# Letting the groups of an edge sort share lines by adding into zeroed memory

## The reference

```
h = emb; acc = emb                      # emb: 12501 x 128
for _ in range(2):
    h = segment_sum(adj_val[:, None] * h[adj_col], adj_row, num_segments=N)
    acc = acc + h
graph = acc / 3
combined = graph[items] + item_features[items]
seq_hidden = take_along_axis(combined, alias_inputs[..., None], axis=1)
... masked mean, tanh, sigmoid, a weighted sum: sess_emb (512 x 128)
scores = (12 * l2norm(sess_emb)) @ l2norm(graph).T
```

## Time and profile before

| | us |
|---|---|
| median of three runs | 4053.59 |
| the profiled execution | 4058.68 |
| its span, first to last instruction | 4056.9 |
| POOL busy | 2797.3 |
| DVE busy | 3050.2 |
| PE busy | 2694.8 |
| ACT busy | 810.4 |

### The profile page before, as it was taken

One profiled execution on the slowest core, in us unless ns is written; L12 is line 12 of the kernel. 1 busy time (PEld: TensorE's weight loads), 2 busy tenths in 40 slices (PEclk: granted clock), 3 DMA queues, 4 the chain that ended last, 5 costly groups with the idle time before them and its releaser, 6 DMA issues.

```text
span 4056.9 us, 81702 instructions
## 1 busy us (share of the span) xinstructions
PE 2694.8 (66%) x14549; PEld 2317.8 (57%) x14550; DVE 3050.2 (75%) x7307; ACT 810.4 (20%) x2729; POOL 2797.3 (69%) x2868
## 2 busy tenths in 40 slices
PE   4899999566656655655664666666556555665798
PEld 2777777455555555655554555555556555553454
DVE  8999999777777777776766677677677776777575
ACT  0899999100000000000000000000000000005453
POOL 2466767777777777777775777777777777775770
PEclk8888888777777777777777677777776777776798
DMA  1000000122222222222243222222222222243243
GB/s 36 3 4 3 3 3 3 51 56 56 56 54 54 55 56 53 56 55 54 56 109 110 56 56 55 56 55 56 56 55 55 55 55 54 55 118 103 61 154 143
DMA packets 153127, 231.39 MB, mean 57 GB/s; under 512 B 65824, under 2 KB 106168, under 8 KB 152568
## 3 DMA queue, kind: packets, MB, share of 16 engines
q0 software_dynamic: 89760, 164.71, 17.6%
q1 hardware_dynamic: 48140, 59.06, 4.7%
q10 hardware_dynamic: 14796, 3.77, 0.9%
HBM read 186.08 MB, written 41.29 MB: 56 GB/s over the span
## 4 chain that ended last, share of the span: by engine, by line
POOL 33%; DMA 24%; issue 22%; DVE 10%; PE 9%; ACT 2%; SPq 0%; ACTq 0%; DVEq 0%; POOLq 0%
POOL store L634 31%; DMA store<-in_L_rec_emb,store 13%; DMA store<-table,store 10%; PE bank L1661 2%; ACT big L708 2%; DVE store L980 1%; PE bank L1602 1%; POOL store L661 1%; DVE big L924 1%; PE bank L1689 1%; DVE big L940 1%; PE bank L1648 1%; DVE store L932 1%; POOL sorted_edges L590 1%; PE bank L1502 1%
## 5 line engine op out<-in xcount | busy, mean ns | idle before, releaser
L1602 PE MATMUL bank<-store,shared 128*128 x9952 | 1762.3, 352 | 1151.8 <-POOLq L619 809.8
L1602 PEld LDWEIGHTS bank<-store,shared 128*128 128x128 f32 x9952 | 1646.9, 260 | 1267.2 <-issue 1264.9
L1294 DVE TENSOR_TENSOR acc<-acc,bank 128x256 f32 x2488 | 1034.4, 416 | 812.9 <-PE bank L1602 797.1
L634 POOL DMA_INDIRECT store<-table,store x1146 | 1086.0, 948 | 388.9 <-issue 326.4
L634 POOL DMA_INDIRECT store<-in_L_rec_emb,store x1146 | 1084.7, 947 | 373.2 <-issue 328.4
L1244 DVE TENSOR_SCALAR shared<-bank,mlo,mval 128x256 f32<-128x256 f32 x2488 | 1340.0, 539 | 0.0
L724 ACT COPY mlo<-store 128x24 f32 (+1 forms) x104 | 21.9, 211 | 2845.2 <-PE bank L1602 2120.4
L708 ACT ACTIVATE big<-big 128x68 f32<-128x68 bf16 x1764 | 557.4, 406 | 0.0
L1502 PE MATMUL bank<-big,store 128*128 128x136 f32 x2352 | 438.6, 326 | 57.4 <-DVE store L932 15.3
L590 POOL DMA_INDIRECT sorted_edges<-moved,block_to x313 | 401.5, 1283 | 101.7 <-issue 101.2
L1502 PEld LDWEIGHTS bank<-big,store 128*128 128x128 f32 x2352 | 351.6, 214 | 142.5 <-ACT big L708 122.2
(11 more groups left out here) (254 smaller groups left out, 1486.4 us busy)
## 6 DMA issues: line engine op xcount, KB each, us to landing
store<-in_L_rec_emb SPq DMA_DIRECT2D x3072, 0.5 KB
store<-in_L_rec_emb ACTq DMA_DIRECT2D x3072, 0.5 KB
store<-table SPq DMA_DIRECT2D x3072, 0.5 KB
store<-table ACTq DMA_DIRECT2D x3072, 0.5 KB
scores<-store SPq DMA_DIRECT2D x48, 512.0 KB, 2.7
store<-in_L_rec_emb,store POOLq DMA_INDIRECT x1146
store<-table,store POOLq DMA_INDIRECT x1146
table<-acc SPq DMA_DIRECT2D x7, 896.0 KB, 9.6
```

Source lines behind the costliest of these rows:

```text
L634: pool.indirect_dma_start(msg[:, j % RING, :], None, source, bass.IndirectOffsetOnAxis(m_col[:, j:j + 1], 0)).then_inc(s_g[gi % (T // GRP4 ...
L1294: add = dve.tensor_tensor(acc[:, bass.ds(off, BUCKET)], acc[:, bass.ds(off, BUCKET)], bank[u % PR][:, 0:BUCKET], ALU.add)
L1602: last = pe.matmul(bank[u % PR][:, q * D:(q + 1) * D], onehot[:, u % SR, q * P:(q + 1) * P], msg_flat[:, bass.ds(offs[u], D)], start=True, ...
```

## The change

Scatters add instead of overwriting, and the buffer starts as zeros. Two groups may then use the same line: the slots that are not a group's own receive zeros from it. So only the whole bucket (49 of them) is padded to lines, and not its 19 pieces. Planning is done in another order: first the totals and starts of the buckets, then the offset of each piece (`gofs`), its remainder by 4 (`place_at`), and from these the padded length of the piece inside its group. The following constants change: GT from 1194 to 1174 tiles, NT from 1200 to 1176, NU from 1244 to 1224 passes, NP from 1248 to 1224, the tiles fetched by single rows from 48 to 47. So POOL issues 1174 - 47 = 1127 gathers a layer. NK = 17 and NKL = 7 scatters a group stay, though their formulas now allow for padding at both ends.

```
-    GT = -(-(E + GR * NB * (R - 1)) // P)
+    GT = -(-(E + NB * (R - 1)) // P)
...
-    NK = -(-(SG * C * P + NB * (R - 1)) // (R * P))
+    NK = -(-(SG * C * P + 2 * NB * (R - 1)) // (R * P))
...
-    KEEP = NOWN // 4
+    KEEP = -(-NOWN // 4)
...
-            pool.iota(blank[:, :, 0:1], [[BUCKET, NT], [0, 1]], base=0, channel_multiplier=0,
-                      allow_small_or_imprecise_dtypes=True).then_inc(s_blank, 1)
-            pool.memset(blank[:, :, 1:2], 0.0).then_inc(s_blank, 1)
+            pool.memset(blank, 0.0).then_inc(s_blank, 1)
...
                     pool.indirect_dma_start(slots, bass.IndirectOffsetOnAxis(block_to[:, h, k:k + 1], 0),
                                             moved[:, h, (skip + k) * R:(skip + k + 1) * R, :].rearrange("p r w -> p (r w)"), None,
-                                            bounds_check=NT * P // R - 1, oob_is_err=False).then_inc(s_sct, 16)
+                                            bounds_check=NT * P // R - 1, oob_is_err=False,
+                                            compute_op=ALU.add).then_inc(s_sct, 16)
...
-                own_tile(layer, source, NOWN, 0)
...
-                round_rows(layer, source, NOWN, 0)
...
-                ge(act, s_mm[M - 1], PER * layer + (T // M * (c - 1) if not isinstance(c, int) or c else -(passes_of(NST - 1) // M)))
+                ge(act, s_mm[M - 1], PER * layer + (T // M * (c - 1) if not isinstance(c, int) or c else 0))
...
-            link(dve.tensor_scalar(gpad_i[:, :, :], gcnt[:, :, :], float(R - 1), None, ALU.add))
+            link(dve.tensor_reduce(tot[:, :], gcnt[:, :, :].rearrange("p g b -> p b g"), AX_X, ALU.add))
+            link(dve.tensor_scalar(toti[:, :], tot[:, :], float(R - 1), None, ALU.add))
+            link(dve.tensor_single_scalar(toti[:, :], toti[:, :], -R, ALU.bitwise_and))
+            link(dve.tensor_copy(tot[:, :], toti[:, :]))
...
+            link(dve.tensor_copy(gpad_i[:, :, :], gofs[:, :, :]))
+            link(dve.tensor_single_scalar(gpad_i[:, :, :], gpad_i[:, :, :], R - 1, ALU.bitwise_and))
+            link(dve.tensor_copy(place_at[:, :, :], gpad_i[:, :, :]))
+            link(dve.tensor_tensor(gofs[:, :, :], gofs[:, :, :], place_at[:, :, :], ALU.subtract))
+            link(dve.scalar_tensor_tensor(gpad_i[:, :, :], place_at[:, :, :], float(R - 1), gcnt[:, :, :], ALU.add, ALU.add))
...
+            link(dve.tensor_tensor(place_at[:, :, :], place_at[:, :, :], lstart[:, 0:GR, 0:NB], ALU.add))
```

More of the change, by code:

```diff
@@ L63, in recommender_program @@
     LAST = -(-(COLS + 1 - (GR - 1) * GC) // C)
-    NKL = -(-(LAST * C * P + NB * (R - 1)) // (R * P)) // 2 * 2 + 1
+    NKL = -(-(LAST * C * P + 2 * NB * (R - 1)) // (R * P)) // 2 * 2 + 1
     LCL = NKL * R
@@ L70, in recommender_program @@
     assert GR % 2 == 1 and C == 8 and NB == 49 and 1 < LAST < SG and SG % Q == 0
-    assert SG * C * P + NB * (R - 1) + SKIP * R <= (P - 1) * LC and LC == 2 * (SKIP * R - 2)
-    assert LAST * C * P + NB * (R - 1) + SKIPL * R <= (P - 1) * LCL and LCL == 2 * (SKIPL * R - 2)
+    assert SG * C * P + 2 * NB * (R - 1) + SKIP * R <= (P - 1) * LC and LC == 2 * (SKIP * R - 2)
+    assert LAST * C * P + 2 * NB * (R - 1) + SKIPL * R <= (P - 1) * LCL and LCL == 2 * (SKIPL * R - 2)
     assert (LC - LCL) % (2 * R) == 0 and NKL < NK
     T = 24
-    GT = -(-(E + GR * NB * (R - 1)) // P)
+    GT = -(-(E + NB * (R - 1)) // P)
     NT = -(-GT // T) * T
@@ L95, in recommender_program @@
     NGRP = -(-GT // GRP4)
-    KEEP = NOWN // 4
+    KEEP = -(-NOWN // 4)
     RW = 2 * L * D + D
     LATE, LATE_END = 4, 2
-    assert T % M == 0 and NP - T < NU <= NP and NT - T < GT <= NT - GRP4 and BEHIND > (LATE + 4) * GRP4 and NOWN == GST - 2
+    assert T % M == 0 and NP - T < NU <= NP and NT - T < GT <= NT and BEHIND > (LATE + 4) * GRP4 and NOWN == GST - 2
     def passes_of(c):
@@ L104, in recommender_program @@
     OPEN, NORMS = 5, 8
-    assert NST // 2 - 1 == L // 2 and HALF % AT_ONCE == 0 and NST % 2 == 0 and NOWN % 4 == 0 and GST >= 8 and NST == NOWN + 4
-    assert NT <= N and NST % 2 == 0 and SG % Q == 0 and D == P and 0 < TAIL < P and T % SR == 0 and T % PR == 0 and LEAD <= PR < SR
+    assert HALF % AT_ONCE == 0 and NOWN % 4 == 3 and T * (4 * KEEP + 1) <= NT and GST >= 8 and NST == NOWN + 4
+    assert NT <= N and SG % Q == 0 and D == P and 0 < TAIL < P and T % SR == 0 and T % PR == 0 and LEAD <= PR < SR
     LOOP = 2 * min(NST // 2 - 1, L // 2, NB // 2)
@@ L115, in recommender_program @@
     PC = [NP // 3 * n for n in range(4)]
-    HELD = "a column is held between 0 and N - 1, and an unused slot's is its tile's number, below NT <= N; a line has 512 bytes"
+    HELD = "a column is held between 0 and N - 1, and an unused slot's is 0; a line has 512 bytes"
     FITS = "a tile's offset is 256 times the buckets that begin at or before it, less one: 0 to ROWS - 256"
@@ L177, in recommender_program @@
         begun = carve(ring, NK * P)
-        blank = ring[:, at[0] - NK * P:at[0] - NK * P + 2 * NT].rearrange("p (x w) -> p x w", w=2)
+        blank = ring[:, at[0] - NK * P:at[0] - NK * P + 2 * NT]
         assert 2 * NT <= NK * P + GR * NB
@@ L183, in recommender_program @@
         hot_b = carve(ring, NB * GC // 2, BF16).rearrange("p (b t) -> p b t", t=GC)
+        place_at = carve(ring, GR * NB).rearrange("p (g b) -> p g b", g=GR)
         assert at[0] <= RW
@@ L455, in _ @@
                              src[COLS * P:E].rearrange("(p t) -> p t", t=1)).then_inc(s_edge, 16)
-            sp.wait_ge(s_blank, 2)
-            sp.dma_start(slots.rearrange("(p x) w -> p (x w)", p=P), blank.rearrange("p x w -> p (x w)")).then_inc(s_zero, 16)
+            sp.wait_ge(s_blank, 1)
+            sp.dma_start(slots.rearrange("(p x) w -> p (x w)", p=P), blank).then_inc(s_zero, 16)
             sp.wait_ge(s_free, GR + 3)
@@ L887, in _ @@
             dve.wait_ge(s_cst, 15)
-            link(dve.tensor_scalar(gpad_i[:, :, :], gcnt[:, :, :], float(R - 1), None, ALU.add))
+            link(dve.tensor_reduce(tot[:, :], gcnt[:, :, :].rearrange("p g b -> p b g"), AX_X, ALU.add))
+            link(dve.tensor_scalar(toti[:, :], tot[:, :], float(R - 1), None, ALU.add))
+            link(dve.tensor_single_scalar(toti[:, :], toti[:, :], -R, ALU.bitwise_and))
+            link(dve.tensor_copy(tot[:, :], toti[:, :]))
+            link(dve.tensor_tensor_scan(cum[:, :], ones[:, 0:NB], tot[:, :], 0.0, ALU.mult, ALU.add))
+            link(dve.tensor_tensor(start[:, :], cum[:, :], tot[:, :], ALU.subtract))
+            dve.wait_ge(s_zero, 16)
+            link(dve.tensor_copy(gofs[:, 0, :], start[:, :]))
+            for g in range(1, GR):
+                link(dve.tensor_tensor(gofs[:, g, :], gofs[:, g - 1, :], gcnt[:, g - 1, :], ALU.add))
+            link(dve.tensor_copy(gpad_i[:, :, :], gofs[:, :, :]))
[3 more added lines that the diff above has]
+            link(dve.scalar_tensor_tensor(gpad_i[:, :, :], place_at[:, :, :], float(R - 1), gcnt[:, :, :], ALU.add, ALU.add))
             link(dve.tensor_single_scalar(gpad_i[:, :, :], gpad_i[:, :, :], -R, ALU.bitwise_and))
@@ L953, in first_places @@
                 dve.scalar_tensor_tensor(first[:, :], ahead[:, :], 1.0,
-                                         lstart[:, bass.ds(g, 1), 0:NB].rearrange("p o b -> p (o b)"),
+                                         place_at[:, bass.ds(g, 1), :].rearrange("p o b -> p (o b)"),
                                          ALU.add, ALU.add).then_inc(s_rk, 1)
```

## The result

The changed kernel takes 4136.24 us, median of 4 runs (4133.60 to 4142.92), against 4052.25 us for the kernel before beside it. The ratio is 1.0211, interval 1.0199 to 1.0223. The time lies in the predicted range, but on the other side of zero: not 44 us less, but 84 us more. The first of the rivals happened.

What follows compares the result with a forecast made beforehand. POOL's gather pace bounds the layers, DVE the sort. From 4058.68 us: layers -48.1, start and planning -0.5, scatters +5.0 gives 4015.1 profiled; 5.1 lower for the median, so 4010 us. Range 4000 to 4160.

Steps and rivals of the forecast that it cites:

- The first of the rivals: Sort: the adding scatter's second address list is made in full, POOL becomes the bound; slower, up to 4252 us; chance 33 in 100.
- The scatters: Sort: adding scatters keep each group just inside POOL's 3.3 us slack, so only the sort's end costs, 5.0 us.
- The formula: Cost of adding in the sort: 16 x max(0, 17x + y - 3.3) + 24x + 2y, with 3.3 us of POOL slack a group.
- x: Sort: extra time of an adding scatter on POOL over the plain 0.975 us; taken as 0.15 us.
- the nearest row: The profile's plain scatter, 0.975 us on POOL, which takes the same as a gather within 0.03 us.
- y: End of a sort group: extra landing time of an adding scatter over the 1.24 us waited before; taken as 0.7 us.
- The bound from above, 0.97: Sort: upper end for x, a whole second list of addresses made one after the other, 0.97 us more per scatter.
- the break-even of 0.30: Sort: the x at which adding costs 48.6 us and eats the whole gain; slower from there on.
- The layers: Both layers: 19 fewer gathers each at POOL's pace of 1.269 and 1.262 us, 48.1 us less.
- The rival of DVE's pace: Layers: removed tiles are worth DVE's pace and not POOL's, 31 us instead of 48, 4027 us; chance 5 in 100.
- The start: Kernel start: the strided iota that holds up DVE's shift on line 861 goes, 6.0 us gained.
- Planning: Planning before the sort: added operations, all on the path, cost 5.5 us more.

Runs made afterwards that it cites:

- the plain version: The changed kernel without the addition (no `compute_op`), so each scatter overwrites its lines: 4012.83 us, ratio 0.9902.
- the probe: The changed kernel with most edges left out, scatters of 64 lines or mostly dropped lines, adding in every other group: adding 1.464 us, plain 0.914 at 64 lines.

## Why the prediction was wrong, step by step

**The scatters: the step that failed.** The formula held and its input did not. "For x I take 0.15, near the plain scatter, the nearest row." The runs show 0.58, and y 0.3 in place of 0.7. With these the prediction's own formula gives 16 x (17 x 0.58 + 0.3 - 3.3) + 24 x 0.58 + 0.6 = 124 us. The first gather came 122.1 us later, with about 3 us gained ahead of the sort; the plain version puts the adding at 123. So the mechanism of the first rival is shown at every point: the slack of 3.3 us a group, the threshold (adding in 5 of 17 scatters is nearly free), and DVE waiting for POOL. Its price is not quite that of its name. It spoke of a second list of addresses made in full, 0.97 us; what is paid is 0.58, nearly fixed for each DMA, and lines twice as long pay it half as often. Why it is 0.58 stays open.

The nearest row misled because it could not bear on the question. That a gather costs as much as a scatter shows that the side addressed has no price; it says nothing of a DMA whose packets are different, and the packet count shows that they are. The bound from above, 0.97, was the only thing known of x, and the break-even of 0.30 lay in the lower third of the range.

On the two rules of the Trainium skill the measurement decides so. The Trainium skill's page "DMA: Bandwidth & Descriptors", section "Anatomy of one DMA — SWDGE (gpsimd) path", calls descriptor generation small and variable; that does not hold for adding scatters here, where 0.58 us on each is 60 % of a plain one. That the number of lines hardly shows does agree with it: from 64 to 128 lines it is 0.08 us more for a plain scatter and 0.11 for an adding one. The Trainium skill's page "Collectives: The Full Stack", section "The bandwidth ceiling: the fold count and why AG ≠ RS ≠ AR", says that an adding transfer needs two read descriptors where a copy needs one; it says so of the reduce step between cores, and here it pointed the right way, since adding has a price. But no run shows a doubled list: the price is 0.6 of a plain scatter, and the packets went from 16 to 128, one for each line.

**The layers.** Forecast 48.1 us less, measured 20.6 + 19.7 = 40.3 from first to last gather. The count of gathers fell as forecast, and the missing 8 us are the pace: 1126 intervals at 1.2725 and 1.2657 us, 0.003 to 0.004 more each than before, which is 3.5 and 4.3 us. It is not the chance of one trace. The five kernels here with 1146 gathers took 1451.8 to 1453.4 us in the first layer and 1443.5 to 1445.0 in the second; the changed kernel, the one with plain scatters and the one in which a fifth add, with 1127 each, took 1432.6 to 1433.4 and 1424.8 to 1426.2. A gather taken away brought about 1 us, not the 1.27 of the mean pace. Why stays open.

Row 0 is not the reason. The changed kernel has at most 1174 x 128 - 150,000 = 272 empty slots, where the kernel before had 2832; the zeroed fill alone left the pace at 1.268 and 1.261 us; and at the end of the changed kernel's first layer the DMA share is 0.20, not 0.53:

```profile
2270.00:2297.00 27.00, 15.89 (x87) 14.36 (x87) 18.77 (x52) 0.00 (x0) 20.49 (x22) 0.75 0.20 53
```

POOL's waits for landed rows do not explain it either. They grew from 36.7 and 30.4 to 47.6 and 36.3 us, but with lines of 8 slots, at a pace of 1.270 and 1.263 us, they are 37.6 and 29.1. The rival of DVE's pace, 31 us, does not fit: it misses by 9 us to the other side. The last part, after the last gather, was 6.1 us shorter, which the prediction did not have. It took 387.5 us in the kernel before and 382.2 in the one with the contiguous iota, whose layers do the same work, so no cause in the change is needed for it.

**The start.** Forecast 6.0 us less. The row that answers to line 861 is

```profile
10.02 2.05 POOL L575 MEMSET store<- 128x2352 f32 x1
10.70 2.03 DVE L859 TENSOR_SCALAR big<-big 128x1248 int32<-128x1248 int32 x1 [7.47 <-DMA big<-in_L_rec_adj_val]
```

and the first count starts at 13.61 instead of 21.65, 8.0 us earlier. The mechanism was right (DVE ends 0.66 us after POOL again). The fill was quicker than forecast, 2.05 us for 2352 neighbouring words and not 3.5 at the rate of the strided ones. And the operation behind the shift gained too, which the forecast did not have: a conversion of the same 1248 columns took 1.72 us beside the strided fill of line 577 and takes 0.81 now that nothing runs beside it.

**Planning.** Forecast 5.5 us more. The loop's first operation starts at 102.94 instead of 105.91, 3.0 us earlier; with 8.0 gained at the start, planning grew by 5.1 us. Right.

**The sum.** With 0.58 and 0.3 for x and y the prediction's sum would have been 4015.1 - 5.0 + 124 = 4134 us for the profiled execution, which took 4135.43. That it fits so closely is partly luck: the layers brought 8 us less than forecast, and the start and the part after the last gather 2 and 6 us more.

## What to carry to other kernels

Treat an operand that changes what a DMA does (here `compute_op`) as a new instruction with a price of its own, which the rows of the plain one need not show; work out the price at which the change stops paying and compare it with the whole range that is left open. Where a cost is paid for each DMA and the engine that issues them has little slack, make the transfers fewer and longer before giving up the idea: with 9 adding scatters of 64-byte lines instead of 17 of 32, the same change is 40 us faster instead of 84 slower. And look at what padding fetches: give empty slots rows of their own.

## What the runs showed of the hardware that was not expected

- An adding scatter by GpSimd held POOL 1.555 us where a plain one took 0.975, with 128 or 64 lines, 32-byte or 64-byte ones, dropped or not (1.46 to 1.57 against 0.91 to 0.99). With 128 lines it left 128 data packets where the plain one left 16.
- At the end of a layer whose last tiles are empty, the gather with which the chain leaves the layer landed in 7.18 us where all its slots ask for one row and in 2.42 where they ask for different ones, at a DMA share of 0.53 and of 0.20. In the probe, where most slots are empty, the first layer's 1127 gathers took 1889 us instead of 1433, at a DMA share of 0.67 in its later part (1400 to 2600 us).
- An integer shift on DVE that takes 0.8 us alone was held until 0.66 us after POOL's instruction beside it, in four kernels: iotas of 9.14 and 13.14 us, fills of 2.05 and 2.10 us.
